# Down product of the 42-row FFN chunk over all 128 rows

## What is computed

```python
I = 938
def _swiglu(x, gate_up, down):
    h = jnp.einsum('bsd,fd->bsf', x, gate_up)
    g, u = jnp.split(h, 2, axis=-1)
    return jnp.einsum('bsi,di->bsd', jax.nn.silu(g) * u, down)
...
out = _swiglu(x, shared_gate_up, shared_down)
...
for e in range(E):
    y = _swiglu(x, experts_gate_up[e], experts_down[e])
    out = out + cw[..., e:e + 1] * y
```

## Time and profile before

| | us |
|---|---|
| median of 3 runs (771.95 to 773.84) | 773.7 |
| the profiled execution | 773.72 |
| its span, first to last instruction | 771.9 |
| PE busy | 670.5 (87%), 3026 matmuls |
| DVE busy | 562.6 (73%) |
| ACT busy | 432.4 (56%) |
| POOL busy | 375.0 (49%) |
| granted PE clock, mean | 0.931 |

### The profile page before, as it was taken

How to read it: one execution, slowest core, us unless ns; L and a number is a source line. 1 busy time by engine, 2 the same in 40 slices (tenths; PEclk the granted TensorE clock), 3 DMA queues, 4 the chain that set the end, 5 groups by cost and what they waited for, 6 DMA issues and landing times.

```text
span 771.9 us, 11929 instructions
## 1 busy us (share of the span) xinstructions
PE 670.5 (87%) x3026; PEld 503.4 (65%) x3026; DVE 562.6 (73%) x1233; ACT 432.4 (56%) x822; POOL 375.0 (49%) x299
## 2 busy tenths in 40 slices
PE   5778989999998999887689999999999999999910
PEld 2456766776675666665467777777777777777700
DVE  4878978879797987987646676666766676666637
ACT  3457656575756658563435565555656555555600
POOL 1324544738456464727236482928255272922245
PEclk9797989999999989989889999999999999999965
DMA  8303001000000000000320303121302203110045
GB/s 260 91 1 97 28 2 36 17 27 28 27 28 27 17 10 27 28 27 29 104 63 14 117 26 117 61 94 30 117 18 67 89 18 117 29 34 22 27 146 191
DMA packets 41301, 44.61 MB, mean 58 GB/s; under 512 B 8052, under 2 KB 31976, under 8 KB 41280
## 3 DMA queue, kind: packets, MB, share of 16 engines
q1 hardware_dynamic: 36672, 35.89, 15.4%
q0 software_dynamic: 4608, 8.47, 3.3%
HBM read 31.62 MB, written 13.76 MB: 59 GB/s over the span
## 4 chain that ended last, share of the span: by engine, by line
PE 52%; DVE 25%; issue 13%; POOL 4%; ACT 3%; DMA 2%; DVEq 1%; POOLq 0%; SPq 0%; ACTq 0%
PE PS L619 48%; PE PS L622 4%; DVE al L1277 3%; DVE prod L1270 2%; DVE acc L1290 2%; POOL pair L505 1%; DVE PS L1270 1%; DVE yT L1380 1%; DVE wd L1363 1%; POOL sorted_dram L515 1%; DVE diag L1367 1%; DMA result_dram<-y_rows,aux_d 1%; DVE dB L1314 1%; DMA stage<-result_dram 1%; ACT y_sb L995 1%
## 5 line engine op out<-in xcount | busy, mean ns | idle before, releaser
L983 ACT ACTIVATE sg<-PS 128x512 f32<-128x512 f32 x216 | 129.0, 598 | 143.5 <-PE PS L619 139.8
L619 PE MATMUL PS<-xh,w_lo 128*128 128x512 f32 x405 | 176.8, 437 | 11.6 <-DVE prod L1270 7.7
L1270 DVE TENSOR_TENSOR PS<-PS,sg 128x512 f32<-128x512 f32 (+1 forms) x160 | 111.4, 697 | 103.4 <-PE PS L619 71.3
L578 POOL DMA_INDIRECT result_dram<-y_rows,aux_d x80 | 77.9, 974 | 177.3 <-DVE y_rows L1645 147.2
L619 PE MATMUL PS<-xl,w_hi 128*128 128x512 f32 x405 | 163.0, 402 | 0.0
L619 PE MATMUL PS<-xh,w_hi 128*128 128x512 f32 x405 | 162.6, 402 | 0.0
L515 POOL DMA_INDIRECT sorted_dram<-h,slot x64 | 73.9, 1154 | 90.1 <-DVE slot L1477 64.2
L619 PEld LDWEIGHTS PS<-xh,w_lo 128*128 128x128 f32 x405 | 78.3, 193 | 44.4 <-DVE prod L1270 14.7
L619 PE MATMUL PS<-ah,w_lo 128*128 128x512 f32 x216 | 96.3, 446 | 4.4 <-ACT ah L991 4.2
L1277 DVE TENSOR_TENSOR al<-PS,ah 128x512 fp32r<-128x512 f32 x140 | 95.7, 684 | 5.1 <-ACT ah L991 2.1
L991 ACT CAST ah<-PS 128x512 fp32r<-128x512 f32 (+1 forms) x160 | 92.9, 580 | 10.3 <-DVE PS L1270 9.8
(11 more groups left out here) (225 smaller groups left out, 1118.4 us busy)
## 6 DMA issues: line engine op xcount, KB each, us to landing
stage<-in_w_gu SPq DMA_DIRECT2D x18, 448.0 KB
xin<-sorted_dram SPq DMA_DIRECT2D x20, 260.0 KB, 2.7
stage<-in_w_dn SPq DMA_DIRECT2D x9, 448.0 KB
tab<-mods_dram SPq DMA_DIRECT2D x8, 384.0 KB, 3.5
sorted_dram<-pad SPq DMA_DIRECT2D x8, 260.0 KB
out<-X SPq DMA_DIRECT2D x4, 512.0 KB, 3.2
stage<-result_dram SPq DMA_DIRECT2D x3, 512.0 KB, 4.8
result_dram<-y_rows,aux_d POOLq DMA_INDIRECT x80
```

The costliest lines, as they stand in the source:

```text
L578: pool.indirect_dma_start(out=result_dram, out_offset=bass.IndirectOffsetOnAxis(ap=aux_d[:, r:r + 1].bitcast(U32), axis=0), in_=y_rows[:, ...
L619: return nc.tensor.matmul(out, lhsT, rhs, start=start, stop=stop, **k)
L983: A.activation(dst, src, ACT.Silu).then_inc(s["silu_done"], 1)
L1270: V.tensor_tensor(product_in(where, c)[0:n, :], bank("up", where, c)[0:n, :], sg[0:n, c % 3, :], ALU.mult).then_inc(s["prod_done"], 1)
```

## The change

`down` is changed for c == SHORT alone. Both of its matmuls take all 128 partitions of the weights and of ah, where they took 42 and 106. The first of them (w_lo by ah) moves behind the wait for the low part, since it now reads partitions 64 to 105 too, which that step writes. Number, columns and order of the matmuls stay as they are. Of the rows that are added, 42 to 63 and 106 to 127 have zero weights; in the first matmul the rows 64 to 105 have the second copy of the low weights, so that the product of low part and low weights, which was left out before, is added as well.

```diff
@@ -662,8 +662,6 @@
                 out, w0 = bank("down", where), DOWN + part_of(c) * P
                 if c != SHORT:
                     high_part(out, buf, w0, ah[:, c % 3, :], c == 0)
-                else:
-                    mm(out, w_lo[buf][0:FL, w0:w0 + P], ah[0:FL, c % 3, :], False, False)
                 if where is WIDE:
                     pe.wait_ge(s["al_ready"], I * FC + c + 1 - (FC - CUT) * (G - 1))
                 elif c < CUT:
@@ -673,7 +671,8 @@
                 if c != SHORT:
                     last = low_part(out, buf, w0, al[:, c % 3, :], c == FC - 1)
                 else:
-                    last = mm(out, w_hi[buf][0:HALF + FL, w0:w0 + P], ah[0:HALF + FL, c % 3, :], False, False)
+                    mm(out, w_lo[buf][:, w0:w0 + P], ah[:, c % 3, :], False, False)
+                    last = mm(out, w_hi[buf][:, w0:w0 + P], ah[:, c % 3, :], False, False)
                 if c == FC - 1:
                     last.then_inc(s["y_bank_done"], 1)
                 elif c < FC - 3:
```

## The result

| | before | changed |
|---|---|---|
| median, us | 773.77 (4 runs, 771.95 to 773.85) | 766.66 (4 runs, 766.43 to 769.23) |
| ratio, 95% interval | | 0.9921 (0.9896 to 0.9947) |
| the profiled execution, us | 773.72 | 766.81 |
| its span, us | 771.9 | 765.0 |
| PE busy, us | 670.5 | 659.7 |

A forecast was written before the change was run, and what follows sets the result against it. PE was taken to bound the expert stage, engine hand-offs the shared stage. Gains of 5.0 us (expert stage), 0.4 (last shared group) and 0 (looped groups) made 5.4 us less, 768.3 us, range 764.3 to 771.4.

The forecast's parts named there:

- The excess of 0.41 us and its cause: Expert tiles and last shared group: the 42- and 106-row pair costs 0.41 us extra because the row count changes.
- All of it goes: At the edited pair: with 128 rows each step becomes 0.23 us, so nothing of the 0.41 us remains.
- The moved wait costs nothing: First matmul waiting for the low half: 0 in experts and last shared group; hidden behind prod in looped groups, 0.
- 20 pairs on the path: 19 expert tiles and the last shared group carry the saving on PE's chain: 8.2 us at the most.
- What is late next: Two-tile experts: ACT's wait for result writes through POOL and DMA eats 2.5 us, plus 0.3 us at one more.
- the prediction's fourth pair: Two-tile expert where ACT came just in time at 505.70: between 0 and 0.55 us eaten, 0.3 taken.
- The sum: Whole kernel: expert stage 5.0, last shared group 0.4, looped groups 0; 5.4 us less, 768.3 us.
- (a): Rival, 13%: nothing holds the gain back, all 20 pairs pay 8.2 us, 765.5 us; 764.1 with the looped groups.
- (b): Rival, 12%: raw load and result writes collide in three more experts, or half the drain stays; 2.9 us gained, 770.8 us.
- (c): Rival, 9%: the gap belongs to place or operands, not rows; nothing gained, 773.7 to 775.1 us.
- (d): Rival, 4%: new PE idle time brings a lower-clock stretch, 1.8 us, in each of 7 looped shared groups; 780.9 us.

The follow-up runs named there:

- e1: Changed kernel with the pair's first matmul over 65 rows and the second over 106; 766.46 us, ratio 0.9913 to the kernel before.
- e2: Changed kernel with the pair's first matmul over 64 rows, the second over all 128; 770.56 us, ratio 0.9942 to the kernel before.
- e7: Kernel before (rows 42 and 106) with only the first matmul moved behind the wait, timed a second time; 771.89 us, ratio 0.9996.
- e9: Kernel before with the wait moved and full rows only in the seven looped shared groups; 771.66 us, ratio 0.9992.
- e10: Changed kernel with full rows only in the last shared group and the 19 expert tiles; 768.07 us, ratio 0.9918 to the kernel before.
- e8: Kernel before, unchanged, timed against itself; 771.35 us, ratio 0.9976.
- e3: Kernel before (rows 42 and 106) with only the first matmul moved behind the wait, first timing; 770.86 us, ratio 0.9978.
- e4: Changed kernel, unaltered, timed once more for its clock; 766.24 us, ratio 0.9884 to the kernel before.
- e11: Changed kernel with ACT's routing-column copies and their wait moved behind the last high part and xh copy; 760.32 us, ratio 0.9827 to the kernel before.

## Why the prediction was right, point by point

- **The excess of 0.41 us and its cause.** Right in size (0.43 in the chain's stretch, 0.44 per undisturbed tile), and the number of rows is the cause (e1, e2). "Weight loads cannot run ahead over such a change" was argued; the trace shows it, as the loads at 485.72 and 486.15 start with their matmuls and not a step ahead. Whether the late load or the emptying of the array makes the gap, no run parts.
- **All of it goes.** Right: the steps are 0.90 us together.
- **The moved wait costs nothing.** Right in the experts. In the looped groups PE waits 0.22 us for it, forecast as a start at 187.95 instead of 187.57, and prod still decides. The working was a little short: the second matmul started 0.34 us behind the first (186.95 to 187.29), not 0.23. e7 and e9 show no effect.
- **20 pairs on the path.** Right as to place (e9, e10). The last shared group gave 0.3 us against the 0.4 put down: 28.85 us before and 28.56 now from one turn_result start (transposes of y_sb) to the next.
- **What is late next.** The mechanism was right, the term a little small. It was 2.5 + 0.3 = 2.8 us; the eight lengths should have gained 3.28 and gained -0.09, so 3.4 us were eaten. The step that was mis-sized is the prediction's fourth pair, the third in time, for which I took 0.3 us because ACT had come just in time (505.70): it grew from 34.73 to 34.93, so 1.0 us was eaten. ACT's wait there was 1.00 us, and its first length lost 0.4 as well, since the writes of the tile before also landed late (0.77 us at 486.64); no raw load runs there (from 480 to 488 us DMA moved 34 GB/s, from 497 to 504 284), and why they did is not shown. That ACT came just in time was one execution's luck: in e8, the same kernel, it waited 0.64 us there, and 0.29 to 0.76 in e2, e3, e7 and e9.
- **The sum.** Expert stage forecast at 5.0 us less: it was 6.3, of which 1.5 is the clock in the first tile, so 4.7. With 0.7 ahead of it the profiled span fell by 6.9, the median by 7.1. Of that 0.7 the last shared group explains 0.3; the rest is less than what this part varies by from one profile to the next. The forecast of 5.4 us lies inside the interval, which is 4.1 to 8.0 us, and 768.3 is 1.6 above the median. The 1.5 us by which the 6.9 of the span exceed it are the size of the clock's part in the first tile, which by e4 the change does not bring each time. The other 18 tiles gained 4.3 us where 18 x 0.41 - 2.8 = 4.6 was forecast, and by that measure the forecast was nearer than the medians say.
- **The rivals.** (a) is what e11 brings about, not the change; e11 also takes away the waits that stood there before. (b) did not come. (c) fell with e1 to e3, and the argument for it was a misreading: the pair is not the only place with partial rows. Each of the 8 groups of the attention part has four matmuls over 16 rows (pqT, 128 columns). At 252.83 to 254.2 us of the kernel before, the step into the first is 0.52 us where the one ahead of it is 0.43; then come 0.21, 0.11, 0.11, and 0.20 and 0.21 going back to 128 rows, where such steps are 0.11. That is again some 0.4 us too much, with other operands and at another place, so the trace alone spoke for the rows. In (d) the price of 1.8 us for a stretch at the lower clock was about right, but my case against it ("such a fall costs little there") was wrong, as the last section shows; the change brought no more of them: of the five full looped groups between two turn_result starts, four were long before and four after.

## What to carry to other kernels

Look at the distance between starts on both sides of a matmul over few rows, not at its duration: one over 42 or 64 rows among full ones costs an extra 0.4 us here, and padding it with zero weights takes that away: to 65 rows most of it, to all 128 the rest, at no cost. Before counting such a gain, follow what the faster engine will meet: a chain on other engines of fixed length (26.6 us here) eats it whole where it already binds. A wait for a slow transfer belongs behind all that does not need the transfer, in a queue that runs in order; moving two small copies gave nearly as much as the change itself.

## What the runs showed of the hardware that was not expected

A stretch at the lower clock costs a looped group of the shared stage 1.6 to 2.5 us, though PE waits for others there. Windows of the kernel before, cut at the starts of its turn_result (group length, PE busy, clock):

```profile
201.11:244.91 43.80, 39.41 (x196) 0.96 0.08 24
244.91:289.57 44.66, 40.90 (x196) 0.92 0.07 24
289.57:331.75 42.18, 37.77 (x196) 1.00 0.08 25
```

The same 196 matmuls took 42.18 us where the clock stayed at 1.00 and 43.80 or 44.66 where it fell. In every profile of this study all but one or two of the five such lengths last 43.8 to 44.7 us and the rest 42.2. Near the end of the slowest group, and then of the fastest, from the last matmul of one product over the transposes of h and the four matmuls of c_exp to the first matmul of the next (start, duration):

```profile
283.46 0.63 PE L619 MATMUL PS<-al,w_hi 128*128 128x512 f32 x1
283.89 1.05 PE L622 MATMUL PS<-mats,h 128*128 128x128 f32 x4
284.74 2.77 PE L619 MATMUL PS<-c_exp,mats 128*128 128x512 f32 x4
286.94 0.80 PE L619 MATMUL PS<-ah,w_lo 128*128 128x512 f32 x1
```

```profile
327.07 0.39 PE L619 MATMUL PS<-al,w_hi 128*128 128x512 f32 x1
327.31 0.65 PE L622 MATMUL PS<-mats,h 128*128 128x128 f32 x4
327.80 1.88 PE L619 MATMUL PS<-c_exp,mats 128*128 128x512 f32 x4
329.12 0.80 PE L619 MATMUL PS<-ah,w_lo 128*128 128x512 f32 x1
```

From the first row to the last it is 3.48 us at the lower level and 2.05 at the higher, and in the slow group the chain runs over PE here. In both groups PE had waited for DVE shortly before; why the clock fell in one and not in the other, no run here shows. The first expert tile (16.9 or 18.4 us) and the last shared group (26.6 to 27.0 or 28.6 to 29.0 us, in kernels of both row counts; 28.85 at a mean clock of 0.82 before, 27.00 at 0.94 in e2) differ in the same way.

The run times show how much of the spread this is. Of the 76 runs of the kernel before that were timed beside the experiments, the 22 with a mean granted clock up to 0.922 have spans of 772.1 to 777.5 us, and the 50 with 0.928 or more 768.6 to 773.0, median 770.5. So one kernel's time moves by some 4 us with the clock that it is granted, and the median of a dozen runs with how many of them met the lower level, which fits e3 and e8. The ten runs of e2 had a median clock of 0.934 against 0.926 of the runs beside them, which fits its low median; that this is all of it is not shown.
